# A decoder of two layers on one core: leaving out the passes of an identity on TensorE between the steps

## The reference, cut to what matters

```python
x = LN(x + scan(sigmoid(x@w_in)*x, exp(-8*softplus(a)*sigmoid(x@w_a))))   # recurrence over 512 tokens
x = LN(x + windowed_attention(q=x, k=ctx, v=ctx))       # 16 heads, windows of 128
x = LN(x + proj(gelu(fc(x))))                           # fake-quantised weights with LoRA
x = LN(x + alibi_attention(x))                          # 16 heads, 512 x 512 scores, clamped bias
x = LN(x + masked_attention(q=x, k=ctx, v=ctx, mask) )  # softmax, then times group_prob
x = x + causal_latent_attention(rms(x));  x = LN(x + moe(rms(x)))   # 8 experts, 2 for each token
```

## Time and profile before

| what | value |
|---|---|
| median of 3 runs | 1497.46 us |
| lowest, highest | 1493.69, 1497.62 us |
| span of the profiled execution | 1493.0 us |
| lowest time less that span | 0.7 us |
| TensorE busy (share of the span) | 1369.8 us (92%) |
| VectorE busy | 1085.1 us (73%) |
| ScalarE busy | 795.1 us (53%) |
| mean granted TensorE clock | 0.969 |

### The profile page before, as it was taken

How to read it: one execution, slowest core, us unless ns; L and a number is a source line. 1 busy time by engine, 2 the same in 40 slices (tenths; PEclk the granted TensorE clock), 3 DMA queues, 4 the chain that set the end, 5 groups by cost and what they waited for, 6 DMA issues and landing times. The chain is left out here.

```text
span 1493.0 us, 29555 instructions
## 1 busy us (share of the span) xinstructions
PE 1369.8 (92%) x9483; PEld 763.5 (51%) x9519; DVE 1085.1 (73%) x2623; ACT 795.1 (53%) x1507; POOL 156.6 (10%) x185
## 2 busy tenths in 40 slices
PE   6878989999999999999999999999999989889990
PEld 3556566664454544443353343343545445578990
DVE  5786744457664777789999999998868877563325
ACT  5375755536647666665455465555666545323332
POOL 1101011100100100001010000000000003224223
PEclk8799999999999999999999999999999989999996
DMA  6223323301402542434343333122222231676754
GB/s 230 79 68 102 104 48 86 86 26 27 127 23 80 163 122 52 137 94 121 104 143 98 93 123 86 51 65 53 62 53 56 52 105 57 206 292 194 213 182 179
DMA packets 124482, 158.32 MB, mean 106 GB/s; under 512 B 31372, under 2 KB 103820, under 8 KB 122348
## 3 DMA queue, kind: packets, MB, share of 16 engines
q1 hardware_dynamic: 120930, 147.06, 33.9%
q0 software_dynamic: 3408, 9.38, 1.7%
HBM read 66.38 MB, written 29.44 MB: 64 GB/s over the span
## 5 line engine op out<-in xcount | busy, mean ns | idle before, releaser
L1668 ACT ACTIVATE prob<-ps 128x512 f32<-128x512 f32 (+3 forms) x832 | 404.0, 550 | 202.8 <-PE ps L1441 108.1
L1960 DVE TENSOR_REDUCE mx<-ps 128x1 f32<-128x512 f32 (+3 forms) x512 | 281.3, 585 | 80.3 <-PE ps L1409 42.4
L1441 PE MATMUL ps<-of_expert 99*128 99x512 bf16 (+4 forms) x768 | 252.4, 357 | 8.2 <-DMA of_expert<-mrow 3.3
L1441 PEld LDWEIGHTS ps<-of_expert 99*128 99x128 bf16 (+1 forms) x768 | 73.1, 98 | 95.5 <-ACT prob L1668 35.7
L1476 PE MATMUL ps<-prob,va 128*32 128x512 f32 (+3 forms) x1024 | 117.0, 530 | 0.2
L1407 PE MATMUL ps<-of_expert 120*128 120x512 bf16 x256 | 92.0, 380 | 3.6 <-DVE mx L1960 0.4
L1401 PE MATMUL ps<-of_expert 96*128 96x512 bf16 x256 | 86.7, 381 | 6.2 <-DVE mx L1956 5.3
L1956 DVE CUSTOM_DVE_ANT_0 ps<-ps,room_a 128x512 f32<-128x512 f32 x128 | 86.1, 710 | 5.5 <-PE ps L1401 5.2
L1956 DVE CUSTOM_DVE_ANT_0 ps<-ps,room_b 128x512 f32<-128x512 f32 x128 | 85.9, 708 | 1.7 <-PE ps L1401 1.4
L1398 PE MATMUL ps<-of_expert 96*128 96x128 bf16 (+3 forms) x256 | 72.4, 306 | 9.0 <-DVE mx L1960 7.3
L1658 ACT ACTIVATE mrow<-ps 12x512 bf16<-12x512 bf16 x64 | 37.2, 581 | 77.3 <-PE ps L1423 77.2
(11 more groups left out here) (251 smaller groups left out, 2550.4 us busy)
## 6 DMA issues: line engine op xcount, KB each, us to landing
of_expert<-parts SPq DMA_DIRECT2D x384, 128.0 KB, 2.4
sorted<-zeros SPq DMA_DIRECT2D x27, 650.0 KB, 7.7
room_a<-in_w SPq DMA_DIRECT2D x30, 512.0 KB, 4.1
otc<-oraw SPq DMA_DIRECT2D x256, 32.0 KB, 2.0
room_b<-in_w SPq DMA_DIRECT2D x15, 512.0 KB, 4.2
ct<-in_c SPq DMA_DIRECT2D x8, 512.0 KB, 3.8
of_expert<-in_w SPq DMA_DIRECT2D x8, 512.0 KB, 8.2
wa<-in_attention SPq DMA_DIRECT2D x4, 768.0 KB, 5.0
```

Of the source, the lines that this page charges most:

```text
L1441: i = pe.matmul(dst[:, lo:S], ks[0:rows, h, t], qs[0:rows, h, lo:S], start=(a != MASKED), stop=(a != CAUSAL and not fixed))
L1668: act.activation(prob[:, quad % PROBS, n, lo:S], key_bank(*st)[:, lo:S], ACT.Exp).then_inc(s_exp, 1)
L1960: i = dve.tensor_reduce(mx[:, slot, s, n:n + 1], src[:, 0:width], AX.X, ALU.max)
```

## The change

`ORDER` is the planned order itself, without `fill()`:

```diff
-ORDER = fill(_order, _ready, _runs)
+ORDER = _order
```

## The result

| kernel | median us | runs | ratio to before (95% interval) |
|---|---|---|---|
| before | 1496.15 (1493.69 to 1497.62) | 4 | |
| with the change | 1504.58 (1502.82 to 1506.76) | 4 | 1.006 (1.0043 to 1.0077) |

A forecast was written before the change was run, and what follows sets the result against it. TensorE was taken to set the pace, hand in hand with VectorE in masked units. Returned time -1 and clock +10 make +9, less about 1 swallowed by later idle time: +8 us, 1505.5 us, range 1502 to 1512.5.

The forecast's parts named there:

- Term 1, the returned time: Ten blocks whose next step follows directly: taking out their passes returns 0 to 6 us, taken as -1 us.
- the passes were in the way: Rival: the ten blocks with a direct successor are all on the path; 6 us returned, no new spell, 1491.5 us; chance 0.10.
- Term 2, which stretches fall: Six thin stretches before dense work, at 106 to 1068 us: five fall to half clock; smaller candidates add 0.5 us.
- Term 2, the price: Each half-clock spell of 3.3 or 6.6 us costs 1.1 to 3.3 us, taken as 1.9; term 2 totals +10 us.
- Term 3: Rest of the kernel: other queues' rows don't move, nothing is released early and no new wait comes; no added time.
- VectorE absorbs the lag: Rival at 674, 772, 871: lag absorbed or few spells, +3 us, 1500.5; chance 0.25 together with no clock effect.
- Spells breed spells: Rival: lagging TensorE delays VectorE and ScalarE, smaller places fall too; ten spells at 2.5 us, 1521 us; chance 0.13.

The follow-up runs named there:

- the fuller plan: Before with the filled share of planned gaps raised from 0.6 to 0.95 and up to 110 passes per block instead of 40: 1492.63 us, ratio 0.9980.
- the fitted one with the ten: Before with block lengths fitted to its trace's idle times, the ten blocks with a direct successor keeping their passes (1077 passes): 1495.68 us, ratio 0.9989.

## Why the prediction was right

The time, the direction and the size were as forecast: +8 us predicted, +8.4 measured. That the passes hold the clock up, and that its falls are what the change costs, is borne out by the runs. That the sum met the size so closely is luck: the sum holds better than its terms.

**Term 1, the returned time (-1 us).** The ten blocks cost nothing that can be measured; taking them out returned nothing (1.0009, 0.9992 to 1.0025), and the spell behind 1225 us got twice as long. The interval still holds the -1 us of the term, so its sign is open; what is out is its far end, -6. What I overlooked is that a block that delays its successor is also activity in a thin stretch. The rival "the passes were in the way" is refuted by that run and by the one with one pass in each block.

**Term 2, which stretches fall.** Of the six places, 674, 772, 871, 1068 and 153 fell, as forecast, and 106 too (a spell of 3.4 us behind 108.0). That part is shown by the stretches after, and these six spells hold 31 us, as counted. But I called the rest small. Over all runs the difference is 150 - 92 = 58 us, and in the two traces it is 68. There the other half lies at the start (10 us more ahead of 100 us), at 1186 (3), in the routing step (3), behind 1279 (10), in the expert stage (7) and at the end (3). The mean clock was to be about 0.96 and was 0.946 to 0.953.

**Term 2, the price.** I took 1.9 us for a spell of about 5 us, 0.37 us for each us at half clock. Measured in the masked units it was 0.15 (0.50 of 3.3), 0.15 (0.48 of 3.3) and 0.21 (1.41 of 6.7) in the kernel with these units bare. Over the whole program it is 8.4/58 = 0.15. The term that was mis-sized is the cost of a spell: its lower bound, 1.1 us for a short one, came from a causal unit, 0.57 against 0.84 of VectorE's time, and a short spell in a masked unit measured 0.5. It was one stretch, applied to units whose VectorE share is another. The masked rows show what happens in its place: VectorE stays busy for 3.30 of 3.30 us while TensorE runs at half clock, so only part of what TensorE loses reaches it. So about twice the half-clock time at about 0.4 of the price came out at the predicted sum. The reason that I gave for staying below half of the spell, TensorE waiting for others inside it, is not in the rows either: it was busy for 6.45 of 6.60 and for 3.30 of 3.30 us. The rule that the penalty is half of the throttled time, from the Trainium skill ("TensorE: Matmul & The Clock Gate", section "HAM oscillation — how this bites in real kernels"), would, as an estimate, make 29 us of these 58 us. This case measured 8.4 us.

**Term 3.** Right: busy times of the other engines are unchanged, and one pass with all the waits (1.0083) is as slow as none.

**The rivals.** That VectorE absorbs the lag is half true, and by the busy times it is the likely reason for the low price; it is not true to the end, since each masked unit still lost 0.5 to 2.0 us. "Spells breed spells" is not shown: the half-clock time is twice my count, but passes are missing at those places too, and no run tells a spell that another brought on from one of its own.

**What stays open.** Where the changed kernel loses the other half of its 8.4 us. The middle is 3.4 us in its trace; the first and last columns sum to 7.8 us there, but to -3.3 us in the kernel with the last 12 blocks and to 3.8 us in that with one pass in each. Timing points at the short blocks outside the middle (only long blocks: 1.0048), but which block does it cannot be read from one execution each. Half-clock time alone does not settle it: the first 17 blocks and the last 12 each take away 20 us of it and bring no time back that these runs can tell. Nor do the runs settle whether the fuller plan really beats the fitted one with the ten: at equal clock it is 1.9 us further below its own before, and the intervals overlap (0.9963 to 0.9997, 0.9976 to 1.0001).

## What to carry to other kernels

A block of useless matmuls in a gap is worth its place when the next step waits for another engine anyway: no run showed a cost of such a block, and it saved about 0.15 to 0.2 us for each us of half clock that it prevented in the masked units and over the whole program. The price of a slow clock was small where VectorE was busy throughout, so price it from a step that occurs once in a unit, in two traces, and not from the clock's ratio. Fill the gaps nearly up (0.95 of the planned length, with up to 110 passes in a block, gained 0.2%), but not gaps that are hardly there: 122 blocks gave the same clock as 48 and lost 4.4 us against them.

## What the runs showed of the hardware

The time of this kernel in one run goes with its clock. Over 203 runs of all the kernels the span is 1479 us + 0.17 for each us of half-clock time, with a correlation of 0.84; in the 80 runs of before alone the slope is 0.24 and the correlation 0.67. A correlation does not say which of the two leads, and over all kernels the passes change along with the clock. And the same passes in the same places do not fix where the spells come. The kernel with the first 17 blocks has the same passes as before up to 499 us, and its trace still has a spell of 3.4 us behind 307 us, where before has none, with 2.4 us of lag behind it (0.7 to 3.1). The kernel with only the long blocks has one at the same place of the program (301.4 us, with 5.7 us less of lag), so the places are not arbitrary. The spread of time is 10 us in 32 runs of before (1491.81 to 1501.92 us), so a lag in a thin region of one trace is not yet a finding.
